# Eight-core transformer layer: who centres the first weight chunks, and the order of the work ahead of the first attention step

## What is computed

```python
def _L0_attn_ref(x, W_qkv, b_qkv, q_gamma, q_beta, k_gamma, k_beta, W_out, b_out):
    qkv = (x @ W_qkv + b_qkv).reshape(b, s, 3, H, D).transpose(2, 0, 3, 1, 4)
    q, k, v = (qkv[0], qkv[1], qkv[2])
    q = _layernorm(q, q_gamma, q_beta)
    k = _layernorm(k, k_gamma, k_beta)
    scores = jnp.einsum('bhqd,bhkd->bhqk', q, k) / math.sqrt(D)
    masked = (col > row) | (row - col >= WINDOW)
    scores = jnp.where(masked[None, None], -jnp.inf, scores)
    attn = jax.nn.softmax(scores, axis=-1)
    out = jnp.einsum('bhqk,bhkd->bhqd', attn, v)
    return out.transpose(0, 2, 1, 3).reshape(b, s, e) @ W_out + b_out

def _L0_ffn_ref(x, w_int8, weight_scale, bias):
    w_deq = w_int8.astype(jnp.float32) * weight_scale
    x_q = activation_quant(simple_rms_norm(x))
    return jnp.einsum('bsd,od->bso', x_q, w_deq) + bias

x = _layernorm(x + _L0_attn_ref(...), axis=-1)
x = _layernorm(x + _L0_ffn_ref(...), axis=-1)
```

## Time and profile before

| | |
|---|---|
| median of 3 runs (range) | 570.72 us (570.52 to 570.97) |
| profiled execution | 574.41 us |
| span of its slowest core (core 1) | 572.8 us |
| spans of all cores | 563.3 to 572.8 us |
| TensorE, VectorE, ScalarE, GpSimd busy in the span | 81%, 73%, 66%, 65% |

### The profile page before, as it was taken

The page is one execution under the profiler, slowest core; times in us unless marked ns, Lnnn a source line. Parts: engine busy times, 40 slices in busy tenths (PEclk is TensorE's granted clock), DMA queues, the critical chain, the costliest instruction groups (busy, mean ns, idle before and its releaser), DMA issues.

```text
span 572.8 us, 9817 instructions; the slowest of 8 cores (563.3 to 572.8 us)
## 1 busy us (share of the span) xinstructions
PE 462.2 (81%) x2546; PEld 202.7 (35%) x2546; DVE 419.3 (73%) x690; ACT 377.0 (66%) x542; POOL 374.5 (65%) x425
## 2 busy tenths in 40 slices
PE   0476876787789988899999898889999896787683
PEld 0122333333334433444444333434444333233231
DVE  3385688654556798987776888977778888846895
ACT  1222666666567778877677878876667798563653
POOL 3374678674576788776777778776777877646221
PEclk9867999999999999999999999999999999889999
DMA  8589920997000001332210000121120100042103
GB/s 165 149 175 166 174 74 3 215 201 133 1 1 2 1 19 21 62 92 105 75 74 2 2 19 19 21 93 74 74 75 2 19 20 20 18 148 75 74 0 146
DMA packets 22291, 40.24 MB, mean 70 GB/s; under 512 B 13664, under 2 KB 15968, under 8 KB 20576
## 3 DMA queue, kind: packets, MB, share of 16 engines
q1 hardware_dynamic: 18864, 28.63, 15.4%
q0 software_dynamic: 3376, 11.01, 13.1%
HBM read 39.11 MB, written 8.39 MB: 83 GB/s over the span
## 4 chain that ended last, share of the span: by engine, by line
PE 36%; DVE 20%; issue 18%; ACT 14%; DMA 7%; POOL 4%; DVEq 1%; ACTq 0%; POOLq 0%; SPq 0%
PE d L344 9%; PE d L385 6%; PE ov L449 5%; PE d L410 4%; PE d L398 4%; DMA wv_s<-wv 3%; DVE nrm L661 3%; PE sc L427 2%; ACT zbq L970 2%; DMA xT<-xT 2%; ACT zbk L970 2%; ACT rec L1000 2%; ACT rec L998 2%; PE ov L385 2%; DVE vt L701 2%
## 5 line engine op out<-in xcount | busy, mean ns | idle before, releaser
L1185 POOL TENSOR_TENSOR pT<-pT,cb_s 128x256 bf16<-128x256 bf16 x176 | 151.9, 873 | 65.7 <-ACT pT L990 65.5
L990 ACT ACTIVATE pT<-sc 128x1024 bf16<-128x1024 f32 x136 | 138.3, 1020 | 42.1 <-PE sc L427 41.3
L344 PE MATMUL d<-xT,wqk_s 128*128 128x512 bf16 x464 | 109.5, 378 | 23.9 <-ACT zbq L970 17.0
L449 PE MATMUL ov<-pT,vt 128*128 128x512 bf16 (+1 forms) x448 | 79.4, 300 | 6.5 <-POOL pT L1185 5.0
L344 PEld LDWEIGHTS d<-xT,wqk_s 128*128 128x128 bf16 x464 | 41.2, 97 | 80.3 <-issue 39.1
L1211 POOL TENSOR_SCALAR bd<-kT,hv 128x63 bf16<-128x63 bf16 (+1 forms) x128 | 59.8, 482 | 4.4 <-DVE kT L666 4.4
L385 PE MATMUL d<-wv_s,xT 128*128 128x512 bf16 x224 | 52.8, 378 | 9.0 <-ACT zbk L970 8.9
L1164 POOL TENSOR_TENSOR sqq<-zbq 128x512 bf16<-128x512 bf16 x31 | 36.4, 1174 | 35.0 <-ACT zbq L970 35.0
L449 PEld LDWEIGHTS ov<-pT,vt 128*128 128x128 bf16 x448 | 41.8, 98 | 49.2 <-issue 14.6
L710 DVE TENSOR_TENSOR qa<-ov,rec 64x512 bf16<-64x512 f32 x64 | 43.9, 686 | 19.2 <-ACT rec L1003 18.2
L1218 POOL TENSOR_TENSOR xh<-xh,fb_s 128x1024 f32<-128x1024 f32 x16 | 34.0, 2127 | 34.5 <-DVE q L762 20.8
(11 more groups left out here) (110 smaller groups left out, 756.4 us busy)
## 6 DMA issues: line engine op xcount, KB each, us to landing
xh<-wqk SPq DMA_DIRECT2D x8, 1024.0 KB, 8.0
xh<-x SPq DMA_DIRECT2D x16, 512.0 KB, 3.3
out<-xh SPq DMA_DIRECT2D x16, 512.0 KB, 2.7
xT<-xT POOLq DMA_DIRECT2D x3, 1024.0 KB, 20.8
wv_s<-wv POOLq DMA_DIRECT2D x2, 1024.0 KB, 19.8
wo_s<-wo POOLq DMA_DIRECT2D x1, 2048.0 KB, 22.4
wf_s<-w POOLq DMA_DIRECT2D x1, 2048.0 KB, 18.1
xT<-xT POOLq DMA_DIRECT2D x2, 512.0 KB, 10.0
```

The lines of the kernel that those rows point to most:

```text
L344: m = e.matmul(z_bank(n, i), wqk[:, c, k, i * 128:(i + 1) * 128], xT[g % 2][:, k, :], start=(k == 0), stop=(k == 7))
L449: m = e.matmul(ov[h][:, q0 * 128:(q0 + nq) * 128], vt[:, slot, c, 64 * h:64 * h + 128], pT[k % 4][:, h * 512 + col:h * 512 + col + nq * 12 ...
L990: e.activation(out=pT[k % 4], in_=sc[k % 2], func=AF.Exp).then_inc(s_exp, 1)
L1185: return e.tensor_mul(both(t, c0, c1), both(t, c0, c1), mb)
```

## The change

`ALONE` becomes 4: VectorE subtracts both halves of chunks 0 to 3, and GpSimd's `centre(1)`, `centre(2)` and `centre(3)` are gone. SyncE waits for the first half of `xT[0]` ahead of the load of chunk 1, no longer for the second. VectorE's, TensorE's and GpSimd's programs ahead of the loop are written in another order. The load of `xT[1]` is issued at the start of step 1.

```diff
-ALONE = 1
+ALONE = 4
...
                     e.dma_start(out=cb, in_=d_cb).then_inc(s_const, 16)
-                    e.wait_ge(s_xT[0], 16)
+                    e.wait_ge(s_xT0, 16)
...
             var(1, 0)
             var(1, 1)
+            z(2, 0)
+            z(2, 1)
             e.wait_ge(s_cr, 1)
             shift(0)
-            z(2, 0)
-            z(2, 1)
             v(*v_unit(0))
+            v(*v_unit(1))
             guard(1)
-            v(*v_unit(1))
...
             centre(0)
             centre(1)
-            centre(2)
             keys(0)
             scale_q(0)
             queries(0)
+            centre(2)
             guard_max(0)
-            centre(3)
-            shift_queries(0)
             keys(1)
             scale_q(1)
             queries(1)
+            shift_queries(0)
+            centre(3)
             guard_max(1)
             centre(4)
...
             square(0, 0)
             square(0, 1)
-            centre(1)
             e.dma_start(out=wv[:, :, 0:512], in_=d_wv[:, :, 0:512]).then_inc(s_wv[0], 16)
-            centre(2)
             guard_keys(0)
             square(1, 0)
             square(1, 1)
-            centre(3)
+            guard_keys(1)
             e.dma_start(out=wv[:, :, 512:E], in_=d_wv[:, :, 512:E]).then_inc(s_wv[1], 16)
-            guard_keys(1)
             square(2, 0)
             square(2, 1)
-            e.dma_start(out=xT[1], in_=d_xT[1]).then_inc(s_xT[1], 16)
             centre(4)

             for s in range(NP):
                 n, m1 = chunk(s), chunk(s - 1)
+                if s == 1:
+                    e.dma_start(out=xT[1], in_=d_xT[1]).then_inc(s_xT[1], 16)
```

## The result

The changed kernel takes 567.66 us (median of 6 runs, 566.23 to 568.34), the kernel before beside it 570.85 (6 runs, 570.28 to 572.83). The ratio is 0.992, with a 95% interval of 0.9899 to 0.9941: it is **faster**, as forecast, by 0.8%. The 567.66 lies in the range of 561.3 to 568.3, but 3.4 above the forecast of 564.3, and outside the narrower 561.5 to 566.4 that the forecast held likeliest. The profiled execution of the kernel after took 567.36, with core 5 the slowest.

A forecast was written before the change was run, and what follows sets the result against it. Bound: the core whose step 0 starts last, behind chunk loads and then the value-weight transfer. Core 1: -9.7 ahead of step 0, +1.0 in the loop; timed runs about -6.4, 570.72 to 564.3, likeliest 561.5 to 566.4, range 561.3 to 568.3.

The forecast's parts named there:

- wv0: First half of the value weights, ahead of step 0: issued 5.6 earlier, landing at 41.3, v(0) 1.0 later than TensorE could.
- Load of chunk 1: Ahead of step 0: issued 2.9 earlier, at 13.5, with no loss from sharing; lands at 20.4, not 23.4.
- rival 2: Chunk 1 lands no earlier, sharing with xT[0]; all after moves 2.9 back: 567.2. Rivals 1 to 3 together 0.20.
- Centring alone: VectorE centring chunk 1 without GpSimd: 5.05 from landing to z, against 5.8; z(1) starts at 25.5, 3.7 earlier.
- Keys, queries and chunk 2: VectorE ahead of step 0: pair 0's keys and queries end at 28.8, chunk 2 at 33.9; z(2) at 34.0, 6.1 earlier.
- Rival 1: wv0 becomes the bound, keeping 19.9, with value units at half clock: step 0 at 55.3, time 567.2. Rivals 1 to 3 together 0.20.
- rival 4: Slower: wv0 still lands at 48.9, set by all traffic, and late VectorE costs steps 0 and 1: 571 to 572.7, chance 0.03.
- wv1: Second half of the value weights, issued about 39.5, needed at 57.8, landing 53 to 59.4: charged nothing, at worst 1.6.
- What the loop gives back: Start of the loop: late VectorE brings scale_q(2) 0 to 2 after step 0's start; charged 1.0 (0 to 3.3).
- Rival 3: VectorE's lag goes through whole in the loop, 3.3 and not 1.0: 566.6. Rivals 1 to 3 together 0.20.
- Rival 5: Time ahead of step 0 is not in the end: 570.7. With a gain spent by several rivals, 0.04.
- The sum: Core 1: -9.7 + 1.0 = -8.7; slowest core of timed runs, step 0 at 57.6, about -6.4: 570.72 - 6.4 = 564.3.

The follow-up runs named there:

- e3: Kernel before, with only chunk 1's load issued early, once the first half of xT[0] has landed: 571.72 us, ratio 0.9983.
- e5: The changed kernel, unaltered, timed again on another chip: 567.28 us, ratio 0.9914 to the kernel before.
- e6: Changed kernel with ALONE = 3, so GpSimd takes its half of chunk 3 back: 567.43 us, ratio 0.9911 to the kernel before.
- e7: Changed kernel with ALONE = 5, so VectorE subtracts both halves of chunk 4 too: 567.91 us, ratio 0.9921 to the kernel before.
- e9: Changed kernel with chunk 4 centred inside step 0, behind scale_q(2), not ahead of the loop: 568.58 us, ratio 0.9918 to the kernel before.
- e12: Changed kernel with ALONE = 1, so GpSimd does second halves of chunks 1, 2 and 3 again: 571.57 us, ratio 0.9950 to the kernel before.
- e1: Kernel before, with two unread sums added on VectorE ahead of the loop to make it late: 573.16 us, ratio 1.0005.
- e4: Changed kernel with chunk s + 4 centred in step s and no chunk 4 ahead of the loop: 571.20 us, ratio 0.9978 to the kernel before.
- e2: Kernel before, with only the first half of the value weights issued early, ahead of GpSimd's centre(1): 575.94 us, ratio 1.0055.
- e10: e6 with the second half of the value weights issued ahead of guard_keys(1): 569.09 us, ratio 0.9922 to the kernel before.

## Why the prediction was right in sign and 3.4 off

| step | forecast, core 1 | measured, core 1 |
|---|---|---|
| chunk 1 issued | 13.5 | 13.3 |
| z(1) | 25.5 | 26.24 |
| z(2) | 34.0 | 35.34 |
| wv0 issued, landed | 23.4, 41.3 | 22.69, 37.3 |
| v(0) to step 0 | 9.3 + 0.7 | 9.25 |
| step 0 starts | 51.3 | 48.27 |
| `scale_q(2)` starts, behind step 0 | 51.6 to 53, 0 to 2 | 51.52, 3.25 |
| charged for the loop | 1.0 | 5.1 |

**What bounds the kernel** was read rightly: the span less the start of step 0 was equal on all cores, and bringing step 0 forward did shorten the longest spans.

**Load of chunk 1** was right in direction, e3 shows it alone, and its landing was 0.5 late on core 1 (7.5 for the load, not 6.9). In e3 the mean load was 1.0 longer than before: rival 2 is out in its full 2.9, but a third of it is there. **Centring alone** was right within 0.3: 26.24 - 20.92 = 5.32 from landing to z(1), against 5.05. **Keys, queries and chunk 2** were right in order, with z(2) 1.3 later: behind GpSimd's two squares L623 took 0.65 and not 0.18, and the two subtractions 3.20 and not 2.36.

**wv0** was set to 41.3 and came at 37.3 on core 1. On the eight cores its transfer took 13.0 to 18.6, inside the 13.5 to 19.86 or just below; v(0) waited for it by 2.04 at most (core 6). Rival 1 is out on these cores (in e5 and e6 core 2 goes that way, step 0 at 52.55 and 52.89), and so is rival 4. The fit in the Trainium skill (DMA: Bandwidth & Descriptors, section Anatomy of one DMA) gave an estimated 6.8: the shortest in any run here was 12.8, and 10.4 for the second half, which is as large; the measurement decides. **wv1**, put at nothing, was nothing in the kernel after, where no core waits for it; in step 0 of e7, e9 and e12 the slowest core waits for it, by 3.73, 2.27 and 2.03.

**What the loop gives back** is the step that failed: 1.0 charged, 5.1 measured on core 1, 4.8 on core 5, which set the end (the mean of the eight cores is 3.5). Three terms of it:
- The lag. VectorE came when foretold, 51.52. TensorE came 3 us before it was foretold, so the lag was 3.25 and not 0 to 2. Those 3 us were no gain, since the chain didn't run through the transfer: on core 1 it goes through VectorE from the landing of chunk 1, through z(1), its copy, its square and the root up to 36.8, and from there through VectorE again without a break, up to 53.9. VectorE was busy 26.55 of the 30 us from 20 to 50, against 20.83 before (view by windows, core 1, below).
- The half of GpSimd. In the earlier trace rows stood the kind of operation that it meets, 2.39 beside GpSimd's half and 0.68 without. The forecast used that row where the half goes, at pair 0, and forgot it where one stays, at chunk 4. It met `scale_q(2)` before too (1.99 on core 5), but ahead of step 0; now the whole of it falls behind the start. 1.7.
- The clock. The wait ahead of z(3,1), with the granted clock at the lower of its two levels (1.2 GHz) behind it, costs another 1.3 to 1.7 on cores 1, 2, 4, 5 and 7, and nothing on 0, 3 and 6. It was reckoned ahead of v(0) alone, where there was nothing to pay.

Busy time by stretch, core 1 after; the columns are named in its first line:

```profile
core 1: us, PE busy (x) PEld busy (x) DVE busy (x) ACT busy (x) POOL busy (x), PEclk, DMA share, GB/s
20.00:50.00 30.00, 21.12 (x95) 8.86 (x94) 26.55 (x30) 13.77 (x19) 12.36 (x16) 0.89 0.84 153
```

The idle time of VectorE in step 0 was to take up the rest. In e1 it did: `scale_q(2)` came 4.0 later against step 0 than before, and step 0 grew by 0.9 to 1.1. After the change only the 1.25 ahead of L701 is gone; 1.10 is still there, at 63.87, as a wait for TensorE's guard, which is late itself.

**The rivals.** Rival 3, "the lag goes through whole", named the right place; its 3.3 was too small, and its 566.6 is 1.1 from the measured time. Rivals 1 and 2, at 567.2, are nearer by number alone, for reasons that the traces exclude or cut to a third. Rival 5 is out: what is left behind step 1 is alike in both kernels.

**The sum** was made for a slowest core whose step 0 starts at 57.6. The slowest one after, core 5, starts it at 49.3, 8.3 earlier, and gives back 4.9, where the forecast had 7.4 and 1.0. On core 1 two errors nearly cancel, a step 0 that starts 3.0 earlier than forecast and a loop that takes back 4.1 more; that this core wins 7.7 up to step 1 where 8.7 was forecast is luck. Part of the 3.4 is the start of the sum as well: 570.72 was the median of 3 runs, and the kernel before took 572.9 to 573.75 on the other three chips. No run takes the later issue of xT[1] by itself; step 1, in which it now stands, takes 12.11 to 12.14 on seven of eight cores, and 12.10 or 12.11 before.

Of its own signs the forecast named the one that failed: the span less the start of step 0 is 516.6 on core 1 and 513.6 to 516.6 over the cores, four of them above the 515 at which it called itself wrong.

## What to carry to other kernels

When a wait is taken off one engine's path, follow each other engine up to the same point, and count as gain only what the latest of them allows: the engine to which the work was given is the first candidate. A duration that a row shows stretched beside another engine's instruction belongs to the pair, so look for every place in the new order where the pair meets, not only for the one that the change takes away. A transfer that is issued earlier is paid for by the loads in flight with it; ask which of them is needed next. And read more than the slowest core of one execution: which core it is, and what holds it, changes from run to run.

## What the runs showed of the hardware

- VectorE's operations with two inputs in SBUF and GpSimd's tensor operations take turns by whole instructions, in both directions: 0.68 becomes 2.39 beside a half of 1.90, `bd` 1.77 becomes 2.73 and 3.85 beside one and two subtractions. VectorE's stretched `scale_q` ends 0.54 or 0.55 behind GpSimd's instruction.
- Even a tiny operation with one input does it: L623 (128 x 32) takes 0.18 at best and 0.89 at 43.05 on core 1 after, where it ends at 43.94, right behind the square's 42.85 + 1.04 = 43.89. The sum L621 is not held: at 40.66 on the same core it takes 2.27, as elsewhere, with a square of GpSimd's beside it from 41.85 on.
- The granted clock isn't told by the last wait alone. Behind 3.80 idle the eight matmuls took 3.57, behind 2.67 both 1.89 and 3.11 (cores 0 and 7 after), behind 2.56 (core 4 of e7) 1.89, behind 2.14 (core 3 of e9) 3.39, behind 1.16 (core 1 of e4) 2.94. What decides stays open.
- The same transfer of half the value weights takes 13.0 to 18.6 us on the eight cores of one execution, and where one half was issued early, a chunk load in flight beside it took 14.4 us for 6.5 (e2, core 1), and 14.4 for 8.6 (e10, core 7). In e3 it lands between 39.6 and 47.6, and the later on a core, the later, nearly throughout, step 0 (52.1 to 59.2): part of the spread between cores comes from there.
